# Running the next-to-last graph's last normalisation beside the last graph's layers, and starting the last graph's first collection ahead of the last unit's sums

## The reference

```python
# x: (8, 1500, 64)   adj: (8, 1500, 1500)
def _layernorm(x, axis=-1, eps=1e-05):
    m = jnp.mean(x, axis=axis, keepdims=True)
    v = jnp.var(x, axis=axis, keepdims=True)
    return (x - m) / jnp.sqrt(v + eps)
...
    x = _layernorm(x + _L0_gnn_ref(x, adj, L0_gnn_kernel, L0_gnn_attention_kernel, L0_gnn_attention_kernel_2, L0_gnn_bias), axis=-1)
    x = _layernorm(x + _L1_gnn_ref(x, adj), axis=-1)
    x = _layernorm(x + _L2_gnn_ref(x, adj, L2_gnn_weight, L2_gnn_bias), axis=-1)
    x = _layernorm(x + _L3_gnn_ref(x, adj), axis=-1)
```

## Time and profile before

| what | us |
|---|---|
| median of the three timed runs | 1536.1 |
| lowest and highest of them | 1535.46, 1537.45 |
| the profiled execution | 1531.98 |
| its span, first to last instruction | 1529.9 |
| mean granted TensorE clock, as a share of full speed | 0.946 |
| busy in the span: PE, DVE, ACT, POOL | 1343.7, 1266.8, 1223.3, 1035.5 |

### The profile page before, as it was taken

One profiled execution on the slowest core, in us unless ns is written; L12 is line 12 of the kernel. 1 busy time (PEld: TensorE's weight loads), 2 busy tenths in 40 slices (PEclk: granted clock), 3 DMA queues, 4 the chain that ended last, 5 costly groups with the idle time before them and its releaser, 6 DMA issues. The chain is left out here.

```text
span 1529.9 us, 21041 instructions
## 1 busy us (share of the span) xinstructions
PE 1343.7 (88%) x7296; PEld 675.7 (44%) x7296; DVE 1266.8 (83%) x1490; ACT 1223.3 (80%) x1404; POOL 1035.5 (68%) x562
## 2 busy tenths in 40 slices
PE   2788889998989988999989989999889999899856
PEld 1443334544445544444545544454445444355323
DVE  2677998897888889898888889988898988988864
ACT  1587888887988878898888878988788888888731
POOL 3067777787677776778677776778767776867412
PEclk7898999999999999999999999999999999999978
DMA  6624552434424442425325344245424343200000
GB/s 94 111 34 63 61 79 52 68 41 48 90 43 63 57 65 56 54 61 52 72 62 75 34 49 89 45 60 59 66 62 58 53 47 69 54 15 16 26 10 11
DMA packets 140879, 84.95 MB, mean 56 GB/s; under 512 B 100372, under 2 KB 130522, under 8 KB 140762
## 3 DMA queue, kind: packets, MB, share of 16 engines
q1 hardware_dynamic: 125542, 64.67, 20.1%
q0 software_dynamic: 14160, 18.51, 15.6%
q10 hardware_dynamic: 1072, 0.43, 0.1%
HBM read 103.33 MB, written 21.38 MB: 82 GB/s over the span
## 5 line engine op out<-in xcount | busy, mean ns | idle before, releaser
L533 POOL TENSOR_TENSOR LS<-LS,MB 125x1000 f32<-125x1000 f32 x372 | 860.7, 2332 | 368.2 <-DVE LS L934 272.2
L774 ACT ACTIVATE LS<-Z 126x1000 f32<-126x1000 f32 x576 | 575.1, 1000 | 150.6 <-PE Z L601 149.9
L782 ACT ACTIVATE LS<-LS 125x1000 f32<-125x1000 f32 x576 | 595.8, 1035 | 47.3 <-POOL LS L533 22.5
L920 DVE TENSOR_TENSOR RP<-LS,RP 125x1000 f32<-125x1000 f32 x480 | 575.6, 1199 | 45.0 <-ACT LS L774 19.4
L599 PE MATMUL Z<-AT,BI 126*126 126x500 fp8e4 x1152 | 367.2, 401 | 77.8 <-ACT LS L774 44.2
L601 PE MATMUL Z<-FS,FO 128*125 128x500 f16 x1152 | 348.8, 384 | 0.0
L628 PE MATMUL M<-LS,V 126*18 126x500 f32 x2304 | 315.9, 622 | 8.8 <-ACT LS L782 8.7
L934 DVE TENSOR_TENSOR LS<-LS,MB 125x1000 f32<-125x1000 f32 x204 | 319.9, 1573 | 0.1
L599 PEld LDWEIGHTS Z<-AT,BI 126*126 126x126 bf16 x1152 | 126.8, 138 | 376.6 <-issue 158.2
L683 PE MATMUL M<-AT,XP 125*128 125x500 fp8e4 x756 | 203.4, 378 | 3.6 <-ACTq L821 3.1
L601 PEld LDWEIGHTS Z<-FS,FO 128*125 128x125 f16 x1152 | 162.0, 141 | 92.4 <-issue 9.2
(11 more groups left out here) (133 smaller groups left out, 798.7 us busy)
## 6 DMA issues: line engine op xcount, KB each, us to landing
MB<-row_maxima SPq DMA_DIRECT2D x48, 500.0 KB, 4.1
adj_cast<-in_adj_dram POOLq DMA_DIRECT2D x96, 183.1 KB, 4.5
FO<-PARTS SPq DMA_DIRECT2D x120, 46.9 KB, 2.1
FS<-PARTS SPq DMA_DIRECT2D x120, 46.9 KB, 2.1
XF<-in_x_dram SPq DMA_DIRECT2D x8, 336.0 KB
XA<-in_x_dram SPq DMA_DIRECT2D x8, 336.0 KB
out_dram<-X SPq DMA_DIRECT2D x7, 375.0 KB
AT<-adj_cast SPq DMA_TRANSPOSE x144, 2.8
```

What stands on the lines that cost most here:

```text
L533: nc.gpsimd.tensor_tensor(rows, rows, MB[:P, u % 2, :, :], ALU.subtract).then_inc(sub_pool, 1)
L774: nc.scalar.activation(LS[:PD, q % RL, :, :], banks("Z", q)[:PD], ACT.Prelu, alpha=SLOPE).then_inc(bent, 1)
L782: nc.scalar.activation(rows, rows, ACT.Exp, scale=0.25).then_inc(exps, 1)
L920: nc.vector.tensor_tensor(run, rows, run, ALU.max).then_inc(maxed, 1)
```

## The change

Graph 6's layer 3 is taken out of the loop's tables (`layer_at` skips it) and issued in the end part: `mean` and `centre` behind layer 0's last `low_part`; the squares on ScalarE behind the three copies of layer 0, into slot 0 of the ring `LS` (`OLD_SQ`) and no longer into `XP`; their sum (`old_sums`) behind layer 1's last `low_part`; the power on GpSimd behind the sixth `end_power`; the scaling (`old_scale`) behind layer 2's last `low_part`. The copy of the factors to PSUM falls away. The last graph now has buffers of its own: `XF` for `Y`, `XA` for `X`, `LAST_MEAN` and `LAST_RSTD`, and `scaled(0, 0)` waits for no store. Layer 0's first two `low_part` stand ahead of the last unit's `keep` (at q = 598) and no longer behind chunk 2's `normalise`. On TensorE the wait for the last `keep` no longer stands ahead of all collection: in the first pass it stands ahead of the accumulator that shares its bank with the last unit's sums (`held`), which now comes third.

```diff
--- before.py
+++ after.py
@@ -139,6 +139,9 @@
 
         SQ = XP[:, :, :].rearrange("p t f -> p (t f)").bitcast(f32).rearrange("p (t f) -> p t f", f=F)
         XF = sb("XF", [P, NT, F], f32)
+        LAST_MEAN = sb("LAST_MEAN", [P, NT], f32)
+        LAST_RSTD = sb("LAST_RSTD", [P, NT], f32)
+        OLD_SQ = LS[:P, 0, :, :].rearrange("p h c -> p (h c)")[:, 0:NT * F].rearrange("p (t f) -> p t f", f=F)
         DEG = sb("DEG", [P, NT], f32)
         RDEN = sb("RDEN", [P, NT], f32)
         RSUM = sb("RSUM", [P, ST, 2], f32)
@@ -287,7 +290,7 @@
 
             for l, at in enumerate(steps):
                 b, off = divmod(q - at, SPG)
-                if off == 0 and 1 <= b < B:
+                if off == 0 and 1 <= b < B and (b, l) != (B - 1, 3):
                     return b - 1, l
             return None
 
@@ -457,7 +460,7 @@
             for c in range(NS):
                 sp.wait_ge(end_x, 9 + c + 1)
                 sp.dma_start(out_v[B - 1][:, KK * c:KK * (c + 1)],
-                             X[:, ST * c:ST * (c + 1), :].rearrange("p (q k) f -> p q k f", k=KK)).then_inc(stored, 16)
+                             XA[:, ST * c:ST * (c + 1), :].rearrange("p (q k) f -> p q k f", k=KK)).then_inc(stored, 16)
             for p in range(PAIRS):
                 sp.wait_ge(fs_in[p], 16 * 2 * NF * B)
                 sp.wait_ge(fo_in[p], fo_count(p, B))
@@ -553,13 +556,15 @@
                     load(*load_at(q))
 
             def end_power(l, c):
-                part = RSTD[:, ST * c:ST * (c + 1)]
+                part = LAST_RSTD[:, ST * c:ST * (c + 1)]
                 pool.wait_ge(end_sum, 3 * l + c + 1)
                 nc.gpsimd.tensor_tensor(part, part, NHALF[:, 0:ST], ALU.pow).then_inc(end_rstd, 1)
 
             for l in range(4):
                 for c in range(NS):
                     end_power(l, c)
+                if l == 1:
+                    power(B - 2, 3)
 
 
         @block.tensor
@@ -738,12 +743,15 @@
                     turn_run(u)
 
 
-            pe.wait_ge(kept_seq, 5 * NU)
+            held = place["G", NU - 1] % RZ
+            ring_free(place["G", NU - 1] + 1)
             parts = (YT, O4, REST)
             for l in range(3):
                 for q in range(NS):
                     pe.wait_ge(end_low, 3 * l + q + 1)
-                    for c in range(NS):
+                    for c in (1 - held, 2, held) if l == q == 0 else range(NS):
+                        if l == 0 and q == 0 and c == held:
+                            pe.wait_ge(kept_seq, 5 * NU)
                         if l and q == 0:
                             pe.wait_ge(end_taken, 3 * (l - 1) + c + 1)
                         for m in range(ST * q, ST * (q + 1)):
@@ -875,7 +883,7 @@
 
             def end_highs(l, c):
                 act.wait_ge(end_x, 3 * l + c + 1)
-                nc.scalar.activation(XP[:, ST * c:ST * (c + 1), 0:F], X[:, ST * c:ST * (c + 1), :],
+                nc.scalar.activation(XP[:, ST * c:ST * (c + 1), 0:F], XA[:, ST * c:ST * (c + 1), :],
                                      ACT.Copy).then_inc(end_high, 1)
 
             parts = (YT, O4, REST)
@@ -887,6 +895,10 @@
                     if l:
                         act.wait_ge(end_back, 3 * (l - 1) + c + 1)
                     nc.scalar.activation(parts[c][:, :], end_banks(c)[:, 0, 0:C], ACT.Copy).then_inc(end_taken, 1)
+                if l == 0:
+                    act.wait_ge(weighed, QN // 2)
+                    act.wait_ge(dve_seq, link_of(B - 2, 3, 1))
+                    nc.scalar.activation(OLD_SQ, Y[:, :, :], ACT.Square).then_inc(squared, 1)
 
 
         @block.vector
@@ -1038,40 +1050,40 @@
                 dve.wait_ge(end_back, 3 * l + c + 1)
                 dve.wait_ge(end_x, 3 * l + c + 1)
                 bank = end_banks(c)[:, 1]
-                y, ps = Y[:, ST * c:ST * (c + 1), :], bank[:P, 0:ST * F].rearrange("p (t f) -> p t f", f=F)
+                y, ps = XF[:, ST * c:ST * (c + 1), :], bank[:P, 0:ST * F].rearrange("p (t f) -> p t f", f=F)
                 if l == 0:
                     for k in range(ST):
                         t = ST * c + k
-                        ins = nc.vector.scalar_tensor_tensor(out=Y[:, t, :], in0=ps[:, k, :], scalar=RDEN[:, t:t + 1],
-                                                             in1=X[:, t, :], op0=ALU.mult, op1=ALU.add)
+                        ins = nc.vector.scalar_tensor_tensor(out=XF[:, t, :], in0=ps[:, k, :], scalar=RDEN[:, t:t + 1],
+                                                             in1=XA[:, t, :], op0=ALU.mult, op1=ALU.add)
                 elif l == 1:
-                    ins = nc.vector.tensor_tensor(y, ps, X[:, ST * c:ST * (c + 1), :], ALU.add)
+                    ins = nc.vector.tensor_tensor(y, ps, XA[:, ST * c:ST * (c + 1), :], ALU.add)
                 else:
-                    ins = nc.vector.scalar_tensor_tensor(out=y, in0=ps, scalar=0.5, in1=X[:, ST * c:ST * (c + 1), :],
+                    ins = nc.vector.scalar_tensor_tensor(out=y, in0=ps, scalar=0.5, in1=XA[:, ST * c:ST * (c + 1), :],
                                                          op0=ALU.is_gt, op1=ALU.add)
                 ins.then_inc(end_added, 1)
                 dve.wait_ge(end_added, 3 * l + c + 1)
 
             def centred(l, c):
                 rows = slice(ST * c, ST * (c + 1))
-                y = Y[:, rows, :]
+                y = XF[:, rows, :]
                 before = XA[:, rows, :] if l == 0 else y
                 if l == 0:
                     dve.wait_ge(kept_seq, 5 * (NU - NS + c + 1))
-                step(c, nc.vector.tensor_reduce(MEAN[:, rows], before, AX.X, ALU.add))
+                step(c, nc.vector.tensor_reduce(LAST_MEAN[:, rows], before, AX.X, ALU.add))
                 follow(c)
-                step(c, nc.vector.scalar_tensor_tensor(out=y, in0=MEAN[:, rows].unsqueeze(2).to_broadcast([P, ST, F]),
+                step(c, nc.vector.scalar_tensor_tensor(out=y, in0=LAST_MEAN[:, rows].unsqueeze(2).to_broadcast([P, ST, F]),
                                                        scalar=-1.0 / F, in1=before, op0=ALU.mult, op1=ALU.add))
                 follow(c)
 
             def summed(l, c):
                 rows = slice(ST * c, ST * (c + 1))
-                y, squares = Y[:, rows, :], SQ[:, rows, :]
+                y, squares = XF[:, rows, :], SQ[:, rows, :]
                 step(c, nc.vector.tensor_tensor(squares, y, y, ALU.mult))
                 follow(c)
-                step(c, nc.vector.tensor_reduce(RSTD[:, rows], squares, AX.X, ALU.add))
+                step(c, nc.vector.tensor_reduce(LAST_RSTD[:, rows], squares, AX.X, ALU.add))
                 follow(c)
-                nc.vector.tensor_scalar(RSTD[:, rows], RSTD[:, rows], F * EPS, None, ALU.add).then_inc(end_sum, 1)
+                nc.vector.tensor_scalar(LAST_RSTD[:, rows], LAST_RSTD[:, rows], F * EPS, None, ALU.add).then_inc(end_sum, 1)
 
             def normalise(l, c):
                 if l in CENTRED:
@@ -1081,17 +1093,27 @@
             def scaled(l, c):
                 rows = slice(ST * c, ST * (c + 1))
                 dve.wait_ge(end_rstd, 3 * l + c + 1)
-                if l == 0 and c == 0:
-                    dve.wait_ge(stored, 16 * (B - 1))
-                nc.vector.scalar_tensor_tensor(out=X[:, rows, :], in0=Y[:, rows, :], scalar=F ** 0.5,
-                                               in1=RSTD[:, rows].unsqueeze(2).to_broadcast([P, ST, F]),
+                nc.vector.scalar_tensor_tensor(out=XA[:, rows, :], in0=XF[:, rows, :], scalar=F ** 0.5,
+                                               in1=LAST_RSTD[:, rows].unsqueeze(2).to_broadcast([P, ST, F]),
                                                op0=ALU.mult, op1=ALU.mult).then_inc(end_x, 1)
 
             def low_part(l, c):
                 rows = slice(ST * c, ST * (c + 1))
                 dve.wait_ge(end_high, 3 * l + c + 1)
-                nc.vector.tensor_tensor(XP[:, rows, F:2 * F], X[:, rows, :], XP[:, rows, 0:F],
+                nc.vector.tensor_tensor(XP[:, rows, F:2 * F], XA[:, rows, :], XP[:, rows, 0:F],
                                         ALU.subtract).then_inc(end_low, 1)
+
+            def old_sums():
+                dve.wait_ge(squared, 4 * (B - 1))
+                nc.vector.tensor_reduce(RSTD[:, :], OLD_SQ, AX.X, ALU.add).then_inc(dve_seq, 1)
+                dve.wait_ge(dve_seq, link_of(B - 2, 3, 2))
+                nc.vector.tensor_scalar(RSTD[:, :], RSTD[:, :], F * EPS, None, ALU.add).then_inc(var_ok, 1)
+
+            def old_scale():
+                dve.wait_ge(rstd_ok, 4 * (B - 1))
+                nc.vector.scalar_tensor_tensor(out=X[:, :, :], in0=Y[:, :, :], scalar=F ** 0.5,
+                                               in1=RSTD[:, :].unsqueeze(2).to_broadcast(bc3),
+                                               op0=ALU.mult, op1=ALU.mult).then_inc(x_ready, 1)
 
             for c in range(NS):
                 low(0, c, end_banks(c)[:, 1])
@@ -1144,11 +1166,14 @@
```

(12 more changed lines are left out.)

## The result

The changed kernel took 1523.22 us (median of 4 runs, 1520.39 to 1524.25) beside 1535.78 us (4 runs, 1534.29 to 1537.45) for the kernel before, in the same comparison: a ratio of 0.9915, with a 95% interval of 0.9900 to 0.9929. The medians differ by 12.6 us, where 9.1 was forecast.

What follows compares the result with a forecast made beforehand. The last 75 us were taken to decide, a chain through VectorE and TensorE's collections. Gains of 5.55 and 3.5 us made 9.1: profiled 1531.98 to 1522.9, plus 4.1 gave 1527.0 us, range 1524.0 to 1530.0.

Steps and rivals of the forecast that it cites:

- What bounds the kernel: Instructions agree up to graph 6's layer 2's last piece, so the last 75 us of 1529.9 decide.
- if the part ahead of 1455 has changed: Sign that the prediction is wrong: a change in the profile before 1455 us, ahead of the last subtractions.
- Part 1: Graph 6's layer 3 leaves VectorE's last five subtractions, which then end 5.55 us earlier.
- Part 2: VectorE's two low parts precede the last `keep`, which starts at 1467.38; chunk 2's low part ends at 1473.38.
- Part 3: TensorE's first collection starts at 1467.02, ahead of the wait for `keep`; chunk 2's matmuls start at 1474.13.
- Rival A: First collection on TensorE runs at full clock: gain 9.8 us, 1526.3 us; chance 0.18.
- The moved work costs nothing: Graph 6's moved layer 3 fits into waits of the end's layers, its store ahead of the final ones: nothing added.
- Rival B: TensorE's clock in layers 1 and 2 differs: plus or minus 2.3 us, 1529.3 or 1524.7; chance 0.17, split evenly.
- C: TensorE can't use the early low parts, so chunk 2's matmuls shift only 5.55 us: 1530.5 us; chance 0.08.
- D: Another engine than VectorE paces the last five subtractions' results, shift under 3 us: 1533 to 1536 us; chance 0.04.
- E: TensorE's clock stays low after the first collection's start, doubling 19.5 us of work: 1546.5 us; chance 0.03.
- the carrying over to timed runs: Final step: the timed median's 4.1 us above the profiled execution is added to 1522.9, giving 1527.0 us.

Runs made afterwards that it cites:

- `old_only`: Changed kernel with the first two low parts and TensorE's wait for the last `keep` placed as before; 1526.45 us, ratio 0.9955.
- `no_old`: Changed kernel with graph 6's layer 3 left out altogether, its store waiting for layer 2's result; 1523.43 us, one execution.
- `after_p4`: Changed kernel, unedited, run again for its profile; 63.6 us from the last Y<-Z,X to the last scaling.
- `after_third`: Changed kernel, unedited, in a third comparison with the kernel before; 1523.83 us, ratio 0.9942.
- `early_only`: Kernel before with only the early low parts and TensorE's early collection, graph 6's layer 3 left in the loop; 1530.86 us, ratio 0.9983.
- `low_no_pe`: Changed kernel with TensorE's wait for the last `keep` back ahead of all collection, low parts left early; 1527.25 us, one execution.

## Why the prediction was right or wrong

**What bounds the kernel: right.** The instructions ahead of the anchor are the same, and all of the change's gain that these runs can tell from scatter lies behind it. One of the prediction's own signs of being wrong did come up, "if the part ahead of 1455 has changed": it was 1.8 us shorter, but it moves as much from one execution of the unchanged kernel to the next.

**Part 1, 5.55 us: right.** Worked out from the anchor, the last subtraction ends 5.97 us behind it; it did (1459.21 - 1453.25 = 5.96). `old_only` has the first collection 5.56 us sooner.

**Part 2, low parts ahead of `keep`: right, to a tenth.** Predicted distances from the anchor: start of `keep` 12.34, end of chunk 2's low part 18.34. Measured: 12.33 and 18.20; GpSimd's small power took 1.01 us instead of 1.11. As forecast, `keep` starts 0.7 us later than it would without the low parts (11.60 in `old_only`).

**Part 3, collecting early: right, 0.2 us too small.** Predicted start 11.98 behind the anchor: 11.98. The 24 matmuls took 1472.10 - 1465.23 = 6.87 instead of 7.11, since the clock rose after 3.4 us and not 4. It could gain more: the changed kernel's other profiles reach the first addition 0.1 to 0.3 us sooner still. Rival A, the full clock from the start, didn't come by itself, although the waits had shrunk; it took throwaway matmuls to get it.

**The moved work costs nothing: right.** `no_old` shows it (61.4 with and without), and VectorE's waits ahead of the additions are 2.90, 5.29 and 3.05 us, where the list of signs had about 7, 5 and 3. The 7 was a slip: it took the moved 1.9 us from the 9.13 of before, though 5.0 of these were TensorE's 24 matmuls still running behind the low part, of which 0.7 are left (1471.45 to 1472.10). The working itself had it, 1475.3 to 1478.2, which is 2.9.

**Rival B** happens in both kernels: layer 2 starts low in one of four profiles before and one of five after, and costs 2.8 us where the prediction had 2.3. Layer 1 started low in all nine; in two of the changed kernel's (`after_p4`, `after_third`) the clock rose within its first eight matmuls, which took 2.71 and 2.77 us instead of 3.5. **C** falls with `early_only` and `low_no_pe`, **D** with the row of five subtractions. **E** did not occur; even in `low_no_pe`, where all three collections began low, the clock came back in each.

**The step that failed is the carrying over to timed runs**, "The median of the timed runs, 1536.1, is 4.1 us above the profiled execution; I carry that over", and with it the range, which allowed for the runs only "the 0.6 us by which the lowest run before lies under the median". The measured time is 3.8 us under the forecast: the timed median lay 2.8 us above the profiled execution and not 4.1, which is 1.3 of it; the part ahead of the anchor was 1.8 shorter; the tail gained 0.4 more than worked out; and 0.3 less lay around the span. The first two, 3.1 us, are no work of the change. Single executions of the unchanged kernel lie anywhere between 1526.9 and 1539.7 us, with a standard deviation of 2.4. So the median of three was itself uncertain by some 1.5 us (an estimate from that deviation), and was 2.4 above the mean of 71; the profiled execution lay 1.7 below that mean, and not 4.1. The median of four runs after it is uncertain by as much. Taken from the mean, 1533.7, the same sum gives 1524.6, and with the 10.2 of all tails and the 0.3 around the span (which was 2.1 us before and 1.8 after) 1523.2: the measured value. The size of the gain was 1.1 us too small in the tail. By the means of the profiles, 0.5 of it came up to the first addition (32.4 to 22.8 us behind the anchor, 9.6 instead of 9.1), 0.4 in layer 1, half of it because the clock rose sooner in two of five, and 0.1 in layer 2, whose shares of low starts happened to differ. The range was made from the mechanism's bounds alone, and lacked a term of about 2 us for the two medians. The gain of 12.6 us in the first comparison was 2 us of luck in the draw on top of 10.6.

Three slips in the working changed nothing in the sum. Six groups of 0.84 us from 1467.02 end at 1472.1 and not 1472.3. Under E, 9.1 of 19.5 us is just under half and not more than half. And the 0.2% that a measurement was said to tell from no change has no run behind it.

## What to carry to other kernels

Work that stands between the last steps of a pipeline and does not feed the end should go behind the end's own waits: here it freed 5.6 us at no cost, and the price of the cover can be checked by leaving the work out. Give the first blocks of a contraction that are ready to TensorE before the last block's inputs are made, and put only the accumulator that shares a bank with data still being read behind the wait; count what this delays on the engine that makes the inputs (0.7 us here). Before forecasting a time from three runs, compare the unchanged kernel with itself: where single executions spread by some us, the baseline's median needs a place in the range, and a distance inside the trace, from a row ahead of the change to the end, measures the change much better than the total.
